# A two-layer decoder on one core: the second layer's loop over the batch unrolled, its shared feed-forward placed inside the next element's block attention, two norms side by side, two row maxima per score step

## The reference, cut to what matters

```python
# block attention, 16 heads of 16, blocks of 64 tokens, causal inside a block
xn = layernorm(h)
q, k, v = split(xn @ Wqkv.T)           # rotary positions on q and k
h = h + softmax(mask(q @ k.T) / 4, inside each block) @ v @ Wout.T
# cross attention, 16 heads of 16, over the 512 context tokens
xn = layernorm(h)
q, k, v = xn @ Wq + bq, ctx @ Wk + bk, ctx @ Wv + bv
h = h + softmax(q @ k.T / 4) @ v @ We + be
# feed-forward: one shared expert, and 16 experts that each choose 256 tokens
xn = layernorm(h)
shared = (gelu(xn @ Sg.T) * (xn @ Su.T)) @ Sd.T
w = softmax(xn @ gate_w.T)             # each expert takes its 256 best tokens
out = h + shared + scatter_add(w * (gelu(xn @ Wg.T) * (xn @ Wu.T)) @ Wd.T)
```

## Time and profile before

| | before |
|---|---|
| median of three runs | 3383.88 us (3381.05 to 3386.18) |
| the profiled execution: time, and span of the trace | 3386.66 us, 3384.9 us |
| TensorE busy, share of the span | 84% |
| VectorE, ScalarE, GpSimd busy | 46%, 33%, 20% |
| mean granted clock of TensorE, 1.0 being 2.4 GHz | 0.889 |
| one pass of layer 1's loop (2377.1 to 2646.3 us) | 269.2 us |
| the four passes | 1837 to 2912 us |

### The profile page before, as it was taken

How to read it: one execution, slowest core, us unless ns; L and a number is a source line. 1 busy time by engine, 2 the same in 40 slices (tenths; PEclk the granted TensorE clock), 3 DMA queues, 4 the chain that set the end, 5 groups by cost and what they waited for, 6 DMA issues and landing times.

```text
span 3384.9 us, 47651 instructions
## 1 busy us (share of the span) xinstructions
PE 2856.0 (84%) x16822; PEld 1667.4 (49%) x16862; DVE 1558.6 (46%) x2519; ACT 1131.8 (33%) x1943; POOL 686.0 (20%) x370
## 2 busy tenths in 40 slices
PE   6769998999899989996897877878788887589997
PEld 3355425642564356432786524523523532368886
DVE  4555366636663567355011561452453344453443
ACT  3564255425442444242232332333233234111111
POOL 0154054405450446044002000000000000012222
PEclk9779998999899989997898788788688779689999
DMA  5340003000300030004784000000100100224542
GB/s 227 143 157 20 1 1 117 20 1 1 113 24 1 1 109 28 1 0 157 258 296 168 14 1 26 13 1 13 26 0 13 26 1 7 87 92 135 170 148 81
DMA packets 64527, 228.15 MB, mean 67 GB/s; under 512 B 12764, under 2 KB 28788, under 8 KB 46808
## 3 DMA queue, kind: packets, MB, share of 16 engines
q1 hardware_dynamic: 46152, 188.44, 15.6%
q0 software_dynamic: 9984, 20.06, 2.4%
q10 hardware_dynamic: 8208, 17.14, 1.4%
HBM read 180.64 MB, written 40.77 MB: 65 GB/s over the span
## 4 chain that ended last, share of the span: by engine, by line
PE 69%; DVE 15%; ACT 7%; issue 5%; DMA 2%; POOL 2%; ACTq 0%; DVEq 0%; another core or an unknown queue 0%; SPq 0%; POOLq 0%
PE psum L549 35%; PE psum L688 7%; PE psum L915 3%; PE psum L1018 3%; DVE arena L1942 2%; ACT arena L1399 2%; PE psum L696 2%; DVE arena L1759 2%; PE psum L1074 2%; PE psum L864 2%; PE psum L836 2%; PE psum L1087 2%; PE psum L1055 1%; PE psum L567 1%; DVE arena L1743 1%
## 5 line engine op out<-in xcount | busy, mean ns | idle before, releaser
L549 PE MATMUL psum<-arena 128*128 128x512 f32 (+7 forms) x4816 | 1292.2, 420 | 97.2 <-ACT arena L1239 25.7
L549 PEld LDWEIGHTS psum<-arena 128*128 128x128 f32 (+1 forms) x4816 | 814.4, 202 | 515.7 <-issue 363.3
L2167 POOL TENSOR_TENSOR arena<-arena 128x1024 f32<-128x1024 f32 x128 | 299.3, 2372 | 143.6 <-DVE arena L1679 140.1
L1679 DVE TENSOR_TENSOR_SCAN arena<-arena,psum 128x512 f32<-128x512 f32 x256 | 291.3, 1201 | 55.7 <-PE psum L688 55.5
L2204 POOL DMA_INDIRECT arena<-xn,arena x36 | 35.5, 985 | 1205.8 <-DVE arena L2103 1151.9
L688 PEld LDWEIGHTS psum<-arena 128*128 128x128 f32 x2048 | 241.1, 197 | 72.3 <-DVE arena L1679 43.7
L688 PE MATMUL psum<-arena 128*128 128x128 f32 x2048 | 252.0, 283 | 27.6 <-ACT arena L1314 27.6
L2174 POOL TENSOR_TENSOR arena<-arena 128x1024 f32<-128x1024 f32 x32 | 75.9, 2372 | 673.6 <-ACT arena L1399 673.6
L1942 DVE TENSOR_REDUCE arena<-psum 128x1 f32<-128x512 f32 x256 | 160.9, 685 | 100.1 <-PE psum L1055 94.1
L1497 ACT ACTIVATE arena<-psum 128x1024 f32<-128x1024 f32 x128 | 129.9, 1023 | 218.5 <-PE psum L1077 218.5
L1759 DVE SCALAR_TENSOR_TENSOR arena<-psum,arena 128x1024 f32<-128x1024 f32 x128 | 156.9, 1245 | 80.4 <-PE psum L825 80.1
(11 more groups left out here) (286 smaller groups left out, 3186.5 us busy)
## 6 DMA issues: line engine op xcount, KB each, us to landing
arena<-in_W SPq DMA_DIRECT2D x48, 1024.0 KB
arena<-c_rows SPq DMA_DIRECT2D x32, 512.0 KB, 3.8
arena<-in_Wg SPq DMA_DIRECT2D x16, 1024.0 KB, 4.9
arena<-in_Wu SPq DMA_DIRECT2D x16, 1024.0 KB, 7.5
arena<-in_Wd SPq DMA_DIRECT2D x16, 1024.0 KB, 9.8
arena<-dl_all SPq DMA_DIRECT2D x5, 1024.0 KB, 5.1
arena<-duT_all SPq DMA_DIRECT2D x5, 1024.0 KB, 7.5
arena<-ut_all SPq DMA_DIRECT2D x5, 1024.0 KB, 9.2
```

Of the source, the lines that this page charges most:

```text
L549: r = mm(dst, w, x, start=i == 0, stop=i == len(pairs) - 1)
L1679: V.tensor_tensor_scan(hs[n % 3][:, c, :], dA[n % 2][:, c, :], bank[4 + c], 0.0, ALU.mult, ALU.add)\
L2167: nc.gpsimd.tensor_tensor(h, h, c_all[:, n % CBUFS, :].unsqueeze(1).broadcast_to([P, 2, L]), ALU.mult)\
```

## The change

**Layer 1 is written out** four times instead of looping, with no meeting point between batch elements. Semaphore waits are on constants.

**The shared feed-forward of element b-1** runs inside the block attention of element b: `ffn_gate` (one pair of projections) before each turn's `weigh_blocks`, the product `ffn_mult` on VectorE, gelu on ScalarE, `ffn_out` in the last turn and after it. The pairs use the banks of the block scores, so `block_scores(p + 2)` waits for the product. The last element's feed-forward stands beside the router's softmax and the threshold search.

**y and norm 0 of element b+1** are done together with norm 2 of element b: two means, two `centre`, two variances and so on, in pairs, in separate banks and buffers. The x tiles have two buffers and are loaded early; the copy `yb` is gone.

**Row maxima.** Query stacks and the first 16 maxima alternate; 20 maxima are ahead of the first score step; then 3, 3 and nineteen times 2 per step. `split_max` moves from a group's end to its fifth step, `take_rows` to its seventh.

**Smaller edits.** Key stacks are cut as 4, 4, 4, 2 (and 2 after `yv`) around norm 1, all stacks are drained by ScalarE, the constant ones of `v1o` are set once, the mask of turn p+1 comes before the sum of turn p, and the expert weights' buffers moved.

```diff
+MAX_AHEAD = 20
+MAX_PER = [3, 3] + [2] * 19
+KS_PARTS = (0, 4, 8, 12, 14, 16)
+FFN_AT, OUT_AT = (2, 4, 6, 4), (6, 7)
...
         @block.tensor
...
-            with pe.Fori(0, B) as b:
+            for b in range(B):
...
+                block_scores(0)
+                if f >= 0:
+                    ffn_gate(f, 0)
+                block_scores(1)
+                for p in range(NC):
+                    transpose_weights(p)
+                    if p >= 1:
+                        transpose_pair(p - 1)
+                    if f >= 0 and p + 1 < NC:
+                        w(mask_done, p + 2)
+                        ffn_gate(f, p + 1)
+                    elif f >= 0:
+                        ffn_out(f, 0)
+                        ffn_out(f, 1)
+                    if f >= 0 and p == 0:
+                        ffn_has(f, 0)
+                    weigh_blocks(p)
+                    if p + 2 < NC:
+                        if f >= 0:
+                            ffn_has(f, p + 1)
+                        block_scores(p + 2)
+                if f >= 0:
+                    ffn_out(f, 2)
                 transpose_pair(NC - 1)
+                if f >= 0:
+                    ffn_out(f, 3)
...
+                for h in range(4):
+                    stack(f"qs{b}", h, sel_q, q_parts)
+                for h in range(4):
+                    act_has(f"qs{b}", h + 1)
+                    for u in range(NC * h, NC * (h + 1)):
+                        scores_for_max(u)
+                    for i in range(4 + 3 * h, 7 + 3 * h):
+                        stack(f"qs{b}", i, sel_q, q_parts)
...
+                    for u in range(MAX_PER[v] if v < len(MAX_PER) else 0):
+                        scores_for_max(n_max)
+                        n_max += 1
...
+                if b + 1 < B:
+                    turn_y(b + 1)
...
+                if more:
+                    w0(y_added, KD * (b + 2))
+                    norm_mean(x_after, 6)
+                dve_has(f"we{b}", 2)
+                norm_mean(x_b, 4)
+                if more:
+                    norm_var(first_norm(b + 1), sq0, 7)
+                norm_var(last_norm(b), sq, 5)
+                if more:
+                    norm_rows(first_norm(b + 1), sd0, 6)
+                norm_rows(last_norm(b), sd, 4)
+                if more:
+                    w0(nb.out, first_norm(b + 1) + 1)
+                    rope_pair(b + 1, 0)
...
-                for m in range(KS):
-                    project(LBA, "sg", m, w_sg, xn)
-                    project(LBV, "su", m, w_su, xn)
...
-                round_end(pe, rd_b, b)
+            dve_has(f"logit{B - 1}", 1)
+            for m in range(KS):
+                if m == KS - 1:
+                    ffn_has(B - 1, 1)
+                ffn_gate(B - 1, m)
+            act_has(f"xn{B - 1}", 2)
+            for i in range(15):
...
                 r.then_inc(cnt_full.sem, 1)
+                if i < NC:
+                    ffn_out(B - 1, i)
...
         @block.vector
...
+                mask_scores(0)
+                for p in range(NC):
...
                     split_step(0, kf, k_parts, p)
+                    if f >= 0 and p >= 1:
+                        ffn_mult(f, p)
+                    if p + 1 < NC:
+                        mask_scores(p + 1)
                     w(bp_ready, p + 1)
```

More of the change, by code:

```diff
@@ L57, in at, with later @@
         return rnd * self.per + (n + self.ahead)
+    def later(self, rounds):
+        s = Sig.__new__(Sig)
+        s.sem, s.per, s.ahead = self.sem, 0, self.at(0, rounds)
+        return s
 class Lane:
@@ L1017, in stack, with key_stacks @@
+                def stack(group, h, select, parts):
+                    t = LBA.fill(pe, 0, group, h)
                     for j in range(3):
                         r = mm(t[0:SR], select[j][:, h % 8, :], parts[j][:, h // 8, :], start=j == 0, stop=j == 2)
-                    r.then_inc(lane.full.sem, 1)
+                    r.then_inc(LBA.full.sem, 1)
+                def key_stacks(n):
+                    for h in range(KS_PARTS[n], KS_PARTS[n + 1]):
+                        stack(f"ks{b}", h, sel_k, k_parts)
@@ L1040, in _ @@
                     r.then_inc(LBV.full.sem, 1)
[L1041 to L1043 removed]
+                key_stacks(4)
                 def scores_for_max(u):
@@ L1845, in _, with w0, centre, norm_factor @@
                     V.tensor_copy(y0[j], bank[4 * j + 3][:, 0:D]).then_inc(wb_free.sem, 1)
-            with dve.Fori(0, B) as b:
+            def w0(s, n):
+                dve.wait_ge(s.sem, s.at(n))
+            def centre(i, dst, src, at):
+                w0(nb.mean, i + 1)
+                for k in range(KD):
+                    V.tensor_tensor(dst[:, k, :], src[:, k, :], bank[at], ALU.subtract).then_inc(nb.cent.sem, 1)
+            def norm_factor(i, factors):
+                w0(nb.sd, i + 1)
+                V.reciprocal(factors, factors).then_inc(nb.rs.sem, 1)
@@ new lines, in norm_apply, with add_y @@
+            def norm_apply(i, dst, src, at):
+                w0(nb.rows, i + 1)
+                V.tensor_tensor(dst, src, bank[at].unsqueeze(1).broadcast_to([P, KD, L]), ALU.mult).then_inc(nb.out.sem, 1)
+            def add_y(b):
+                dve.wait_ge(ld_xB.sem, ld_xB.at(16, max(b, 1)))
+                for k in range(KD):
+                    w0(y_turned, KD * b + k + 1)
+                    V.tensor_tensor(xbs[b % 2][:, k, :], xbs[b % 2][:, k, :], bank[6 + k], ALU.add).then_inc(y_added.sem, 1)
@@ L1874, in pair_out @@
+                for x in range(1, 4):
+                    rope_pair(b, x)
                 def pair_out(p):
```

539 lines of the change are left out of this document (312 added, 227 removed).

## The result

| | before | after |
|---|---|---|
| median of four runs | 3382.47 us (3379.38 to 3386.18) | 3153.74 us (3151.91 to 3157.85) |
| ratio | 1 | 0.9316, 95% interval 0.9301 to 0.9331 |
| profiled execution: time, span | 3386.66 us, 3384.9 us | 3154.66 us, 3152.9 us |
| mean granted clock of TensorE | 0.889 | 0.923 |
| TensorE, VectorE, ScalarE busy | 84%, 46%, 33% | 87%, 49%, 36% |

The change takes 229 us away (232.0 between the two profiled spans).

What follows compares the result with a forecast made beforehand. TensorE sets nearly all the time, through full work, mutual waits with VectorE and ScalarE, and low clock. Gains of 159.7 us from the profiled 3386.66 gave 3227; the median, 2.8 lower, 3224 us; range 3176 to 3272.

Steps and rivals of the forecast that it cites:

- Feed-forward inside block attention: Layer 1, three elements: merging takes 59.9 us of two stretches to 61, net gain 1.6 us each with `wo` starting warm.
- merged stage warm: Rival, chance 0.25: projection pairs keep TensorE at 2.4 GHz through block attention's turns; 40 us less than forecast, 3184 us.
- Norm 2 beside norm 0: Between elements, three times: pairing the norms and dropping the loop boundary saves 19 us each, bounds 13 and 22.
- Score steps: Cross attention, four passes: two maxima per step give pairs of 3.95 us; 71.7 against 80.70, 9.0 us saved a pass.
- Query stacks: Before the cross attention's score steps, four passes: interleaving stacks with first maxima saves 7.0 us each, bounds 4 and 9.
- Norm 1 and `wo`: After block attention: factor rows wait for fewer key stacks, 3.4 us a pass; the output projection starts warm, 2.7 less.
- Last element: Last logits to threshold search: softmax hides under four feed-forward pairs; 15.5 us saved after 2.5 charged for chunks in search.
- Block 0's attention: First element's block attention, without feed-forward inside: the earlier mask saves 1.5 us, bounds 0 and 4.
- Entry: Start of layer 1: early loading of x removes a 4.67 us wait, the y transposes' end replaces it; 3.3 us saved.
- ScalarE's table loads: Merged stage: five more loads a pass of 1.28 us, hidden; a drain per switch, 7 us more in all, left out.
- Instruction supply: Rival, chance 0.03: written-out code is fetched without reuse, costing 224 us if fully exposed, 3448 us, slower than before.
- my boundary term: Loop boundary between elements, three times: 4.1 us of engines waiting for each other and the branch would go.

## Why the prediction was wrong

**The step that failed is "Feed-forward inside block attention": "I take a pair at 6.0, half cold", and with it "TensorE's own work in a turn is about 6.4 us, all at clock 0.50", and the 21 us for what stands behind the last pair.** The first was a guess between 3.5 and 7.6, and the mean pair measured 4.6. The second took the duration of the small matmuls as a property of theirs. It was one of the clock: with pairs between them the weights by values went from 2.42 to 1.44 us and the transposes of the weights, in all turns but one, from 1.97 to 1.09. Piece by piece: from the start to the end of the second pair 10.4 us instead of 12.8; the two turns behind 24.1 instead of 27.4 (12.1 each instead of 13.7); and weighing, transposes and the four `out` chunks 13.6 instead of 21, more than half of the miss, with every chunk at 2.4 GHz (1.90 and 0.61 us). So the stage took 48.1 us instead of 61, three times. That is 39 of the 72 us by which the sum fell short. Not all of it is the clock: the run with the feed-forward alone gives clock and filled waits about equal shares of what the merge gained. Of my rivals "merged stage warm" (46 us) came true to within 2 us; I had given it 0.25. I had also priced it wrongly: by its own rows it gains 59.9 + 2.7 - 46 = 16.6 us an element against before, not 15, and lies 45 us below the forecast, not 40. Measured were 11.9, and 2.6 for the warm `wo` (3.61 us instead of 6.20).

The argument against that rival was "the small matmuls stay at 0.50 even back to back". The observation is right, and it came true in the paired norms too (busy 8.00 of 8.00 us at 0.59). What it could not tell is what happens with dense work close by. The warm case's 3184 us was still 30 too high, which the stages around it make up, the next norms above all.

**Norm 2 beside norm 0**: forecast 19, measured 25.4 (with the rotary stretch, which I had left as it was). The mechanism was right. 17.6 of it is the pairing; writing the loop out alone gave 4 to 5 us a pass; the other 3, with the meeting point among them, were not tried alone. The size was off, as I read it, since two chains interleaved also keep the clock: rotary projections, `v2` and `yk` follow a warm start (2450.48 to 2484.42 us at 0.90, which has the variances' cold spell at its start only). Three times 6.4 is 19 us of the miss.

**Score steps**: forecast 9.0, measured 11.2; pairs of steps took exactly 3.95 us, as worked out (weighings at 2376.47, 2380.42 and 2384.37). My hand-overs were too dear: 1.54, 1.54 and 0.85 us instead of 1.85 each. I also added 2.7 us for cold spells, and three elements show one. **Query stacks**: 7.0 against 6.6. **Norm 1 and `wo`**: 6.1 against 7.3.

**Last element**: 18.0 to the start of the search against 19.3. For the search itself I had charged 2.5 us for the four `out` chunks in the search. The first rounds with a chunk begin 2.50, 2.65, 2.67 and 2.66 us apart, those before the change 2.61 to 2.64: nothing was added, since the counts run in 0.56 us, not 0.97, while a chunk keeps the clock up.

**Block 0's attention**: 1.5 forecast, and 33.29 us measured where it was 33.05. The earlier mask gives nothing: the division comes later and the result transposes wait 1.35 us for it. **Entry**: 3.3, and the first block scores are 3.0 us earlier, which the scatter of layer 0 hides.

**ScalarE's table loads** are hidden, as the sum had it. In the merged stage:

```profile
2309.01 1.28 ACT L1613 ACT_TABLE_LOAD   x1
2310.31 1.06 ACT L1613 ACTIVATE arena<-arena 128x1024 f32<-128x1024 f32 x1
```

The next activation starts 0.02 us after the load, and the one before had ended 0.01 us ahead of it. The Trainium skill, "ScalarE: Activation LUTs", section "What ACT_TABLE_LOAD costs", adds a drain of about 1.38 us to each switch of tables; neither side of the load shows one here.

**Instruction supply** cost nothing that the runs show. The written-out loop alone gave 19 us in the medians and 14.7 from layer 1 on, of which my boundary term held about 12.

The range was too narrow at its lower end, as I read it, for one reason. It took the clock of each stage as an uncertainty of its own, while one cause moves them all: where TensorE waits less, every stage behind is warmer too. Merged stage, rotary stretch, tail and score steps were off to the same side together.

## What to carry to other kernels

A duration read from a trace belongs to the clock at which it ran. When a change takes waits away or brings dense matmuls near small ones, price the small ones at both levels of the clock, and the stages behind as well; a wait that ends in a cold spell costs twice. Where a wait of TensorE can't be removed and dense work is behind it, a few dense matmuls whose result nobody reads can be worth their place: here they gave 23 to 27 us of the 1276 from layer 1 on. Where TensorE is already busy they are worth about what they cost.

## What the runs showed of the hardware

- TensorE can be busy without a gap and fall to 1.2 GHz: 8.00 of 8.00 us busy at a clock of 0.59, in matmuls with one moving column and the factor rows behind them (the clock is 1.00 when the variances start and 0.50 from 2454.00 to 2458.30 us; the trace's ends of matmuls are modelled, and the last idle time that it shows, just ahead, is 0.32 us). With six matmuls of 128x256 among them the clock stays at 1.00, and the stretch is no longer. The Trainium skill, "TensorE: Matmul & The Clock Gate", section "HAM oscillation — how this bites in real kernels", tells of the fall as one of idle gaps; here it is seen without one.
- The end of a hardware loop's pass cost TensorE 4.27, 5.25 and 4.68 us of "issue" with a drain and a meeting, and 2.0 us with both of these and the loop written out.
- Layer 0, with the same code, ended up to 13 us apart between kernels and executions (first block scores at 1867.3 to 1880.7 us). That is more than several terms of this study, and the reason for comparing stretches as well as totals.
